# Adaptive feed-forward kernel on one core: first element loaded without the sort, prologue reordered

## The reference

```python
h = jnp.einsum('bsd,bdh->bsh', x, W[cat_ids]) + b[cat_ids][:, None, :]
w_scale = jnp.mean(jnp.abs(weight)) + EPS
w_quant = jnp.clip(jnp.round(weight / w_scale), -1.0, 1.0)
a_scale = jnp.max(jnp.abs(h), axis=-1, keepdims=True) + EPS
a_quant = jnp.round(jnp.clip(h / a_scale * 127.0, -128.0, 127.0))
out = x + jnp.einsum('bsi,oi->bso', a_quant, w_quant) * (w_scale * a_scale / 127.0)
```

## Time and profile before

| | us |
|---|---|
| median of 3 runs | 524.89 |
| the three runs | 530.56, 524.89, 524.25 |
| profiled execution: its own time | 530.25 |
| profiled execution: its span | 528.5 |
| TensorE busy in the span | 506.0 (96%) |
| VectorE, ScalarE, POOL busy | 366.8, 348.5, 305.1 |
| moved by DMA | 172.76 MB, mean 327 GB/s |

### The profile page before, as it was taken

How to read it: one execution, slowest core, us unless ns; L and a number is a source line. 1 busy time by engine, 2 the same in 40 slices (tenths; PEclk the granted TensorE clock), 3 DMA queues, 4 the chain that set the end, 5 groups by cost and what they waited for, 6 DMA issues and landing times. The chain is left out here.

```text
span 528.5 us, 13752 instructions
## 1 busy us (share of the span) xinstructions
PE 506.0 (96%) x2584; PEld 359.5 (68%) x2585; DVE 366.8 (69%) x652; ACT 348.5 (66%) x504; POOL 305.1 (58%) x397
## 2 busy tenths in 40 slices
PE   4699999999999999999999999999999999999996
PEld 1477677777777666777777776777776667777773
DVE  3297864878667968856866768855978577565844
ACT  3376766777667657767756777757767576567642
POOL 3297654656556566655656556565666666555640
PEclk9799999999999999999999999999999999999999
DMA  5779998999999999999999999989999899899843
GB/s 163 254 290 321 366 324 300 375 384 330 316 338 362 362 334 418 371 322 379 363 305 336 327 358 391 371 301 325 406 345 373 282 391 341 314 319 322 320 152 126
DMA packets 71728, 172.76 MB, mean 327 GB/s; under 512 B 8096, under 2 KB 8224, under 8 KB 64800
## 3 DMA queue, kind: packets, MB, share of 16 engines
q1 hardware_dynamic: 71712, 172.59, 91.9%
HBM read 139.00 MB, written 33.55 MB: 326 GB/s over the span
## 5 line engine op out<-in xcount | busy, mean ns | idle before, releaser
L325 POOL TENSOR_TENSOR sb_xT_lo<-sb_xT_raw,sb_xT_hi 128x512 fp32r<-128x512 f32 x128 | 187.1, 1462 | 188.7 <-PE ps_cond L648 187.4
L646 PE MATMUL ps_cond<-sb_w_hi,sb_xT_hi 128*128 x512 | 223.7, 437 | 3.5 <-ACT ps_cond L363 2.4
L648 PE MATMUL ps_cond<-sb_w_hi,sb_xT_lo 128*128 x512 | 200.5, 392 | 0.0
L647 PE MATMUL ps_cond<-sb_w_lo,sb_xT_hi 128*128 x512 | 199.3, 389 | 0.0
L554 DVE TENSOR_REDUCE sb_absmax<-ps_cond 128x1 f32<-128x512 f32 x128 | 87.8, 686 | 130.7 <-PE ps_cond L648 129.0
L511 DVE TENSOR_TENSOR sb_w_lo<-sb_w_raw,sb_w_hi x106 | 140.3, 1363 | 1.9 <-ACT sb_w_hi L372 1.9
L614 PE MATMUL ps_y<-sb_ffnT,sb_aT 128*128 128x512 bf16 x512 | 131.5, 379 | 2.8 <-ACT sb_aT L417 2.7
L372 ACT ACTIVATE sb_w_hi<-sb_w_raw x106 | 106.2, 1050 | 40.1 <-DMA sb_bias<-cond_b 39.8
L436 ACT ACTIVATE sb_a_rounded<-ps_cond,sb_rounder,sb_a_inv 128x512 f32<-128x512 f32 x128 | 99.5, 777 | 43.1 <-DVE sb_a_inv L560 42.5
L646 PEld LDWEIGHTS ps_cond<-sb_w_hi,sb_xT_hi 128*128 128x128 f32 x512 | 96.6, 189 | 37.9 <-issue 9.6
L648 PEld LDWEIGHTS ps_cond<-sb_w_hi,sb_xT_lo 128*128 128x128 f32 x512 | 96.2, 188 | 21.9
(11 more groups left out here) (72 smaller groups left out, 38.0 us busy)
## 6 DMA issues: line engine op xcount, KB each, us to landing
sb_w_raw<-cond_w SPq DMA_DIRECT2D x53, 1024.0 KB, 6.9
sb_xT_raw<-x_t SPq DMA_DIRECT2D x128, 256.0 KB, 5.1
sb_x_rows<-x SPq DMA_DIRECT2D x128, 256.0 KB, 5.2
out<-sb_x_rows SPq DMA_DIRECT2D x128, 256.0 KB, 4.7
sb_bias<-cond_b SPq DMA_DIRECT2D x54, 256.0 KB, 7.7
sb_ffn_raw<-ffn_t SPq DMA_DIRECT2D x1, 1024.0 KB, 6.8
sb_w_raw<-cond_w SPq DMA_DIRECT2D x4, 256.0 KB, 7.2
sb_cat_row_i<-itok SPq DMA_DIRECT2D x1, 64.0 KB, 3.6
```

What stands on the lines that cost most here:

```text
L325: pool.tensor_tensor(xT_lo[:, m, :], xT_raw[:, m, :], xT_hi[:, m, :].bitcast(F32), ALU.subtract).then_inc(x_lo_done, 1)
L646: pe.matmul(ps_cond, x_hi_k, w_hi_k, start=False, stop=False, skip_group_check=True)
L647: pe.matmul(ps_cond, x_hi_k, w_lo_k, start=False, stop=False, skip_group_check=True)
L648: last_mm = pe.matmul(ps_cond, x_lo_k, w_hi_k, start=False, stop=(k == KD - 1), skip_group_check=True)
```

## The change

- The order: element 0 and its category come first (their keys get -16384 where the category equals that of element 0), the rest stays sorted. With these inputs the first four steps are category 26, then category 0 follows, and a new matrix is needed at steps 0, 4, 9, 10, 13, 15, 16, 20, ... and then at 41, 42, 45, 46, 47, 50, 52, 53, 55, 56, 59, 61, 62 and 65. From step 59 the order is that of before.
- SyncE loads `itok[0]` by itself first (4 bytes), and xT of element 0 at once. VectorE only clamps the category before `first_there`. The four pieces of the first matrix, its bias and then the feed-forward weight follow; then xT of the next element (`next_there`), x of element 0, xT of steps 2 and 3 when the element columns are there, and after the table the look at steps 1 to 5. The load of xT for step 4 now stands behind the look at step 5.
- POOL makes zeros first, and takes the low parts of pieces 0 and 2 of the first matrix; VectorE takes 1 and 3, before and behind its table work.
- ScalarE takes the four high parts first, then the element columns, then the sum over the feed-forward weight, then seeds steps 1 and 2, and only then fills its own table. Step 0 has no seed: VectorE adds its bias into the accumulator bank (128 x 512) before the first row maxima.
- VectorE makes the look-ups of steps 2 and 3 behind the first row maxima and `ternary_begin`.
- TensorE: 20 products of zeros before the table and 4 in it instead of 12 behind it; the product of the sum (`ffn_sum_mm_done`) stands between step 0 and step 1.

Semaphores and tiles that are only declared are left out of the diff, as is the offset arithmetic of L487 to 493, which stays as it is.

```diff
-    BUSY = 12
+    BUSY, BUSY_BEHIND = 20, 4
@@ sync @@
+    sp.dma_start(first_cat_i[:, :], itok[0:1].rearrange("(a b) -> a b", a=1)).then_inc(first_cat_loaded, 16)
     sp.dma_start(cat_row_i[:, :], itok.rearrange("(a b) -> a b", a=1).to_broadcast([P, B])).then_inc(cat_row_loaded, 16)
+    sp.dma_start(xT_raw[:, 0, :], x_t[0, :, :]).then_inc(xT_loaded[0], 16)
     sp.dma_start(cat_col_i[:, :], itok.rearrange("(p a) -> p a", a=1)).then_inc(cat_col_loaded, 16)
-    sp.dma_start(ffn_raw[:, :], ffn_t[:, :]).then_inc(ffn_loaded, 16)
...
     sp.wait_ge(first_there, 1)
...
+    _, (category,) = nc.values_load_multi_w_load_instructions(
+        first_cat[0:1, 0:1], engines=[sp.engine], skip_runtime_bounds_check_because="a clamped category")
     category = bounded(sp, category, C - 1)
-    load_xT(element, 0)
     for k in range(KD):
         sp.dma_start(w_raw[:, k * H:(k + 1) * H],
                      cond_w[bass.ds(category, 1), :, k * H:(k + 1) * H].rearrange("c p f -> (c p) f"),
                      ).then_inc(w0_loaded[k], 16)
-        if k == 0:
-            sp.dma_start(bias[:, 0:H], cond_b[bass.ds(category, 1), :].to_broadcast([P, H])
-                         ).then_inc(bias0_loaded, 16)
-    load_rows(element, 0)
-    sp.wait_ge(elements_done, 3)
-    sp.wait_ge(table_done, 1)
+    sp.dma_start(bias[:, 0:H], cond_b[bass.ds(category, 1), :].to_broadcast([P, H])).then_inc(bias0_loaded, 16)
+    sp.dma_start(ffn_raw[:, :], ffn_t[:, :]).then_inc(ffn_loaded, 16)
+    sp.wait_ge(next_there, 1)
+    _, (element,) = nc.values_load_multi_w_load_instructions(
+        next_element[0:1, 0:1], engines=[sp.engine], skip_runtime_bounds_check_because="an element among 128")
+    load_xT(bounded(sp, element, B - 1), 1)
+    sp.dma_start(x_rows[:, 0, :], x[0, :, :]).then_inc(rows_loaded[0], 16)
+    sp.wait_ge(elements_done, 3)
+    for step in range(2, XT_RING):
+        load_xT(xT_of(step + W_AHEAD - XT_AHEAD), step)
+    sp.wait_ge(table_done, 1)
+    for step in range(1, W_RING):
+        load_w(*row_of(sp, step, NEW, 4), step, None)
     for step in range(W_RING, W_AHEAD):
+        row = row_of(sp, step, NEW, XT_ELEMENT + 1)
         if step == W_RING:
-            sp.wait_ge(w0_lo_done, KD)
-        load_w(*row_of(sp, step, NEW, 4), step, None if step == W_RING else PIECES * (step - W_RING))
+            sp.wait_ge(w0_lo_done, KD // 2)
+            sp.wait_ge(w0_lo_pool_done, KD // 2)
+        load_w(*row[0:4], step, None if step == W_RING else PIECES * (step - W_RING))
+        ahead = step - W_AHEAD + XT_AHEAD
+        if ahead >= XT_RING:
+            sp.wait_ge(x_lo_done, ahead - XT_RING + 1)
+            load_xT(bounded(sp, row[XT_ELEMENT], B - 1), ahead % XT_RING)
@@ gpsimd @@
-    pool.memset(ident[:, :], 1.0).then_inc(consts_done, 1)
-    pool.memset(ones[:, :], 1.0).then_inc(consts_done, 1)
-    pool.memset(rounder[:, :], ROUNDER).then_inc(consts_done, 1)
+    pool.memset(zeros[:, :], 0.0).then_inc(consts_done, 1)
...
-    pool.memset(zeros[:, :], 0.0).then_inc(consts_done, 1)
+    pool.memset(ident[:, :], 1.0).then_inc(consts_done, 1)
+    pool.wait_ge(consts_done, 4)
+    pool.affine_select(out=ident[:, :], in_=ident[:, :], compare_op=ALU.is_equal, fill=0.0,
+                       base=0, pattern=[[-1, P]], channel_multiplier=1).then_inc(consts_done, 1)
+    pool.memset(rounder[:, :], ROUNDER).then_inc(consts_done, 1)
...
+    pool.memset(ones[:, :], 1.0).then_inc(consts_done, 1)
...
-    for step in range(X_AHEAD):
+    split_x_high(0, 0)
+    split_x_low(0, 0)
+    for k in range(0, KD, 2):
+        pool.wait_ge(w0_hi_done, k + 1)
+        pool.tensor_tensor(w_lo[:, k * H:(k + 1) * H], w_raw[:, k * H:(k + 1) * H],
+                           w_hi[:, k * H:(k + 1) * H].bitcast(F32), ALU.subtract).then_inc(w0_lo_pool_done, 1)
+    for step in range(1, X_AHEAD):
...
@@ scalar @@
-    act.wait_ge(consts_done, 3)
-    act.activation(marks[:, 0:1], rounder[:, :], ACT.Abs)
+    act.wait_ge(consts_done, 1)
+    act.activation(marks[:, 0:1], zeros[:, 0:1], ACT.Abs)
+    def w0_high(k):
+        act.wait_ge(w0_loaded[k], 16)
+        act.activation(w_hi[:, k * H:(k + 1) * H], w_raw[:, k * H:(k + 1) * H],
+                       ACT.Copy).then_inc(w0_hi_done, 1)
+    for k in range(KD):
+        w0_high(k)
+    act.wait_ge(consts_done, 8)
     act.wait_ge(elements_mm_done, 1)
     for column, behind in ((XT_ELEMENT, W_AHEAD - XT_AHEAD), (ROWS_ELEMENT, W_AHEAD - ROWS_AHEAD),
...
     act.activation(ffn_abs[:, :], ffn_raw[:, :], ACT.Abs,
...
-    for k in range(KD):
-        act.wait_ge(w0_loaded[k], 16)
-        act.activation(w_hi[:, k * H:(k + 1) * H], w_raw[:, k * H:(k + 1) * H],
-                       ACT.Copy).then_inc(w0_hi_done, 1)
-        if k == 0:
-            act.wait_ge(banks_opened, COND_BANKS - 1)
+    act.wait_ge(table_done, 1)
+    for step in range(1, SEED_AHEAD):
+        (bias_offset,) = row_of(act, step, BIAS_OFFSET, 1)
+        bias_offset = bounded(act, bias_offset, (BIAS_RING - 1) * H)
+        act.wait_ge(w_loaded[step], 32)
+        if step == 1:
+            act.wait_ge(banks_opened, COND_BANKS - 2)
...
-            seed(0, 0)
-    act.wait_ge(table_done, 1)
...
+        seed(bias_offset, step)
+    act.activation(act_table[:, HI_AHEAD - SEED_AHEAD:HI_AHEAD - SEED_AHEAD + B, SEED_OFFSET], table[:, 0:B, BIAS_OFFSET],
...
+    act.activation(act_table[:, 0:B, HI_NEW:HI_OFFSET + 1], table[:, 0:B, NEW:W_OFFSET + 1],
...
-        bias_offset, new, offset = act_row(step)
+        _, new, offset = act_row(step)
...
-        if step > HI_AHEAD - SEED_AHEAD:
-            act.wait_ge(w_loaded[step - 1], 32)
-            seed(bias_offset, step - 1)
...
@@ vector @@
+    dve.wait_ge(first_cat_loaded, 16)
+    dve.tensor_scalar(first_cat[:, :], first_cat_i[:, :], 0.0, float(C - 1), ALU.max, ALU.min).then_inc(first_there, 1)
...
+    dve.wait_ge(consts_done, 5)
+    done()
...
+    begin(dve.scalar_tensor_tensor(key_base[:, :], cat_row[:, :], float(B), free_index[:, :], ALU.mult, ALU.add))
+    begin(dve.tensor_scalar(key_ahead[:, :], cat_row[:, :], cat_row[:, 0:1], -float(2 * C * B), ALU.is_equal, ALU.mult))
+    done()
+    begin(dve.tensor_tensor(key_row[:, :], key_base[:, :], key_ahead[:, :], ALU.add))
+    done()
...
+    begin(dve.tensor_reduce(next_key[:, :], key_row[0:1, 1:B], AX.X, ALU.min))
+    begin(dve.scalar_tensor_tensor(key_own[:, :], key_row[:, :], 1.0, ident[:, :], ALU.mult, ALU.mult,
+                                   accum_out=key_col[:, 0:1]))
+    done()
+    dve.tensor_scalar(next_element[:, :], next_key[:, :], B - 1, None, ALU.bitwise_and).then_inc(next_there, 1)
+    begin(dve.tensor_copy(part_index_bf[:, :], part_index[:, :]))
+    begin(dve.tensor_tensor(cat_start[:, :], key_col[:, :], part_index[:, :], ALU.subtract))
+    begin(dve.tensor_scalar(key_below[:, :], key_row[:, :], key_col[:, 0:1], 0.0, ALU.is_lt, ALU.add,
+                            accum_out=rank[:, 0:1]))
+    done()
+    dve.tensor_scalar(place[:, :], free_index[:, :], rank[:, 0:1], None, ALU.is_equal).then_inc(placed, 1)
+    begin(dve.tensor_scalar(cat_below[:, :], key_row[:, :], cat_start[:, 0:1], 0.0, ALU.is_lt, ALU.add,
+                            accum_out=n_below[:, 0:1]))
+    begin(dve.tensor_scalar(later_cat[:, :], key_row[:, :], -float(B), cat_start[:, 0:1], ALU.add, ALU.is_ge))
...
+    begin(dve.tensor_scalar(cat_col_bf[:, :], cat_col_i[:, :], 0.0, float(C - 1), ALU.max, ALU.min))
+    done()
+    dve.tensor_tensor(is_first[:, :], rank[:, :], n_below[:, :], ALU.is_equal).then_inc(firsts_there, 1)
...
+    def w0_low(k):
...
+    w0_low(1)
+    dve.wait_ge(counts_mm_done, 1)
...
+    dve.sem_inc(offsets_there, 1)
+    dve.wait_ge(table_mm_done, 1)
+    dve.wait_ge(consts_done, 7)
+    dve.tensor_copy(table[:, 0:B, 0:CAT_COLUMNS],
+                    cond_ps[COND_BANKS - 1][0:1, :].rearrange("a (b c) -> a b c", c=CAT_COLUMNS)).then_inc(table_done, 1)
+    w0_low(3)
+    begin(dve.tensor_copy(ident_bf[:, :], ident[:, :]))
+    done()
+    dve.sem_inc(ident_there, 1)
-    for step in range(1, LO_AHEAD):
-        new, offset = w_slot(dve, step)
-        split_low(new, offset, step)
+    new_1, offset_1 = w_slot(dve, 1)
+    split_low(new_1, offset_1, 1)
...
     def ternary_begin():
...
-        if not last or u + LO_AHEAD < U:
+        if not last and not (first and u == 0) or last and u + LO_AHEAD < U:
...
         dve.wait_ge(cond_mm_done, r + 1)
+        if first and u == 0:
...
+            dve.wait_ge(bias0_loaded, 16)
+            dve.tensor_tensor(cond_ps[0][:, :], cond_ps[0][:, :], bias[:, 0:H], ALU.add).then_inc(bias0_added, 1)
+            dve.wait_ge(bias0_added, 1)
...
             ternary_begin()
+            for step in range(2, LO_AHEAD):
+                split_low(*w_slot(dve, step), step)
+            new, offset = w_slot(dve, LO_AHEAD)
...
@@ tensor @@
-    pe.wait_ge(consts_done, 6)
-    for n in range(COND_BANKS - 1):
+    pe.wait_ge(consts_done, 1)
```

(43 more changed lines are left out.)

72 lines of the change are left out of this document (22 added, 50 removed).

## The result

The changed kernel takes 524.03 us (median of 20 runs, 519.70 to 527.63), the kernel before beside it 528.56 us (20 runs, 524.25 to 531.88): a ratio of 0.9922, 95% interval [0.9901, 0.9942]. By the ratio that is 4.1 us less, by the medians 4.5, where 5.4 were forecast. The profiled execution takes 524.48 us (span 522.7); for it the prediction said 524.85. The three runs shown before had a median 3.7 us under that of twenty, and the forecast time of 519.5 us was worked out from it: of the 4.5 us between 519.5 and 524.03, 3.7 come from there.

A forecast was written before the change was run, and what follows sets the result against it. TensorE's beat was taken as the bound, the DMA queue where new matrices lie close. An earlier start gains 6.0 us, the new order costs 0.6: 5.4 off a median of 524.89 gives 519.5 us, range 514.9 to 524.4.

The forecast's parts named there:

- The bound and the beat: All steps: TensorE sets a beat of 3.847 us a step, except where new matrices lie close and the queue sets it.
- Step 0: At the start: 4-byte load in 3.2 us, first piece issued at 4.5, first product near 11, end 11 us earlier.
- Step 1: Behind the first step: waits for the feed-forward weight (landing 15.1) and its sum, starts at 18.2 against 24.8.
- The clock: Between the first two steps: TensorE idles, the clock falls again, so the second step takes 3.9 us; price 1.2 us.
- Step 4: First step with category 0's matrix, issued at 15.6: starts at 28.9 against 34.21, a gain of 5.3 us.
- The new order: Dense stretch, steps 52 to 62: relief lost on the queue costs nothing to 3.4 us; 0.6 taken.
- a stall of over 2 us: Around steps 55 to 62: a stall this long was named as a sign that the prediction is wrong.
- The chances: Whole kernel: forecast 0.50; within 2% 0.92, faster by over 2% 0.06, slower by over 2% 0.02.
- A: Start: faster bias, clock kept up over the wait, dense stretch free; gain 8 to 9 us, time 516.5; chance 0.17.
- B: Category 0's matrix or `ternary_end` 2 us late, or dense stretch costs 3.4; gain 2.5, time 522.4; chance 0.22.
- C: Start: slow pieces delay the feed-forward weight to 26.4 and the second step to 29.5; time 529.6; chance 0.05.
- D: Start: 4-byte load as slow as whole `itok`, first step late by 2 us; time 521.5; chance 0.06.

The follow-up runs named there:

- e5: The changed kernel without the bias loads of steps 1 to 127, every step using the first bias: 515.17 us, ratio 0.9776 to the kernel before.
- e15: The changed kernel measured and profiled again, nothing altered: 523.70 us, ratio 0.9862 to the kernel before.
- e18: The changed kernel measured and profiled once more, nothing altered: 521.86 us, ratio 0.9876 to the kernel before.
- e7: The changed kernel with the feed-forward weight's load ahead of the first matrix and ScalarE's sum ahead of the high parts: 524.73 us, ratio 0.9955.
- e13: The kernel before, run again against itself with nothing altered: 528.18 us, ratio 0.9929.
- e2: The changed kernel with the order of steps of the kernel before: 524.33 us, ratio 0.9934 to the kernel before.
- e16: The changed kernel with the old order of steps, measured again: 526.33 us, ratio 0.9953 to the kernel before.
- e1: The kernel before with only the new order of elements, element 0's category first: 532.58 us, ratio 1.0098 to the kernel before.
- e14: The kernel before with only the new order of elements, measured again: 531.89 us, ratio 1.0021 to the kernel before.

## Why the prediction was right or wrong

- **The bound and the beat**: right. 3.847 us before and after, and with the biases gone (e5) not 0.1 us is lost behind the start.
- **The time**: 519.5 was said and 524.03 measured. 3.7 us of that are the median of three executions from which it was reckoned. The other 0.9 are the gain, 4.5 us of the medians where 5.4 was said.
- **Step 0**: 12.02 where 10.8 to 11 was said (11.68 and 11.43 in e15 and e18). The 4-byte load was far quicker than its lower bound (below), and the first piece was issued at 3.26 and not at 4.5. But its high part began only at 7.09, so it took 3.8 us where 2.7 was taken. And the key chain was slower: `place` took 1.26 us and `key_own` 1.12, against 0.28 for such operations before. Both lay beside a subtraction on POOL; in e7, where they do not, they take 0.28 and 0.47.
- **Step 1**: 16.90 where 18.2 was said; the wait for the sum is what was late next, as forecast. In the first profile its parts are: the last pieces landed by 9.6 (9.3), bias at 5.42 + 5.9 = 11.3 (12.3), the weight at 5.82 + 8.0 = 13.8 (15.1), which ScalarE's sum follows at once:

```profile
13.86 1.91 ACT L421 ACTIVATE sb_ffn_abs<-sb_ffn_raw 128x2048 bf16<-128x2048 f32 x1 [2.27 <-DMA sb_ffn_raw<-ffn_t]
```

- **The clock**: right in two profiles of three, e15 and e18: TensorE waits 2.4 and 2.8 us between steps 0 and 1, and step 1 takes 4.4 us at the low clock (3.9 was said). In the first profile the place was wrong: the wait was only 0.9 us and the clock stayed up; it had fallen before step 0, and the price, about 1.2 us, was paid there (4.0 us from 12.02 to 16.01).
- **Step 4**: 27.97 where 28.9 was said (29.41 and 29.59 in e15 and e18), its matrix issued at 15.92 (15.6). The gain at step 4 was 6.2 us in the first pair of profiles and 4.1 in the second, e15 against e13 (forecast 5.3), at step 8 6.4 and 4.0 (forecast 6.0), and 6.7 without the bias loads. These terms hold within what one execution differs from the next.
- **The new order**: here is the step that failed, a term that was mis-sized. "The 77 steps from step 50 on lost 0.05 us a step; I take 0.6, near the low end", for steps 55 to 62. The mechanism, relief lost on a full queue, fits: the loss is the queue's (e5), and it shows at the steps named, though not in every profile of this order. But the changed kernel loses 2.4, 3.7 and 1.0 us in steps 54 to 64, mean 2.4, where the kernel before loses nothing, and two of the three pass the prediction's own sign of being wrong, "a stall of over 2 us". A part lies at steps 9 to 16, which it did not look at (1.7, 0.0 and 1.8 us; before 0.4 and 0.1): it counted that no matrix is due from 5 to 8 as a gain, and not that three of the next five steps then fall due together. In return less is lost at 38 to 46. Over all steps from 8 to 126 the changed kernel loses 9.0, 6.6 and 4.6 us, and with the old order 3.5 and 5.8 (e2, e16): 2.1 us more in the mean, where 0.6 was taken. In the kernel before, the order alone cost 5.1 and 2.4 us (e1, e14).
- **Luck in the sum**: what the order gives at the start was mis-sized too, and the other way. 0.7 us was taken for steps 5 to 8; with the old order the changed kernel's start is 4.7 and 3.2 us later (e2, e16). The two errors largely cancel, so that the order's net effect in the changed kernel (0.3 us by e2, 2.6 by e16 and e15) and the gain of the profiled execution (5.77 us, 5.4 forecast) came out close. Which stretch makes the medians' gain 0.9 us smaller than forecast, no profile shows.
- **The chances**: this failed as well. 0.92 was for "within 2%", read as no difference, from the sentence that a measurement can tell about 2%. The twenty runs tell 0.8% from no change, and all three comparisons of the changed kernel lay under 1 (0.9922, 0.9862, 0.9876). The forecast of 1.0% was itself a statement that the kernel is faster, and the chances gave it no name: 0.92 covers both "faster by 1%" and "the same".
- **The rivals**: A had the clock up over the wait (so in the first profile), but not its gain. B's dense stretch is nearest to what came: it was to cost up to 3.4 us, and steps 54 to 64 cost up to 3.7; B's gain of 2.5 us did not come. Nor did C (the weight landed at 13.8) or D (the 4 bytes were there at 2.0).

## What to carry to other kernels

An order that moves one group to the front changes where every later load falls due: list the due steps anew, and look first at the stretch right behind the start, where the queue has not caught up. To split "the start" from "the queue", take the cheapest traffic out of both kernels; here that turned 4 us with a wide spread into 6.7 us with almost none. And when a kernel runs at the edge of its queue, compare a kernel with itself before a difference under 1% is believed, and take more than one profile of it: here three profiles of one program put the fall of the clock in two different steps and their starts 1.7 us apart.

## What the runs showed of the hardware that was not expected

The 4-byte load was issued at 0.78 and VectorE used it at 2.00, 1.2 us after the issue began; the bounds had been 2.0 to 3.6. The Trainium skill, DMA: Bandwidth & Descriptors, Anatomy of one DMA, gives about 2.0 us as the fixed cost of a DMA, fitted on DMAs that GpSimd issues; this one was issued by SyncE, and for it the measurement decides:

```profile
0.78 0.37 SPq L220 DMA_DIRECT2D sb_first_cat_i<-itok  x1
...
2.00 0.14 DVE L487 TENSOR_SCALAR sb_first_cat<-sb_first_cat_i 1x1 int32<-1x1 int32 x1 [1.87 <-DMA sb_first_cat_i<-itok]
```

Work on VectorE and POOL at the same time came with longer times on both: a cast on POOL that takes 0.61 us took 2.30 beside `ternary_end`, and two low parts on VectorE 3.85 us against 2.55 to 2.77 later (timeline of the changed kernel):

```profile
22.01 2.33 DVE L573 SCALAR_TENSOR_TENSOR sb_ffnT<-sb_ffn_raw,sb_half_up,sb_ffn_minus 128x2048 bf16<-128x2048 f32 x1
...
22.51 2.30 POOL L338 CAST sb_xT_hi<-sb_xT_raw 128x512 fp32r<-128x512 f32 x1 [0.33 <-DMA sb_xT_raw<-x_t]
...
24.26 3.85 DVE L548 TENSOR_TENSOR sb_w_lo<-sb_w_raw,sb_w_hi  x2
```

The Trainium skill, GPSIMD Engine Reference, Specifications, says that POOL shares its SBUF interface with VectorE, with contention for instructions that have two SBUF inputs or use both ports. The rows of `ternary_end` and of the two low parts agree, as each has two inputs in SBUF. `place`, stretched to 1.26 us beside POOL, has one and a factor for each partition, and no run here shows why it was held. Nor do the profiles say which of two engines held the other.
